# Products with the unit matrix in TensorE's waits, in a twelve-stage decoder

## The chip, the cores and the metric

The kernel runs on one core of a Trainium2 chip. The metric is device time in microseconds (us) of that core, the median of the runs; lower is better. TensorE (PE) multiplies matrices, VectorE (DVE), ScalarE (ACT) and GpSimd (POOL) compute elementwise and reduce, SyncE (SP) issues DMAs. Each engine works through its own list of instructions in order and waits on semaphores for the others.

## The reference

Four decoder layers over x, 64 sequences of 64 positions with 128 channels in float32, each of three parts with a residual. The parts differ from layer to layer:

```
x = x + _L0_attn_ref(_layernorm(x), ...)       # a0: differential attention
x = x + _L0_xattn_ref(ctx_1024, _layernorm(x)) # w0: dynamic time warping onto x
x = x + _L0_ffn_ref(_layernorm(x), ...)        # f0: three trees of experts, then attention
x = x + _L1_attn_ref(_layernorm(x), ...)       # a1: attention, 16 heads
x = x + _L1_xattn_ref(_layernorm(x), ctx_1024, ...)  # x1: attention with a gated memory
x = x + _L1_ffn_ref(_layernorm(x), ...)        # f1: mixture, top 2 of 8, and a shared expert
x = x + _L2_attn_ref(_layernorm(x), ...)       # a2: attention by pooled sums
x = x + _L2_xattn_ref(_layernorm(x), ctx_1024, ctx_1024, ...)  # x2: cross attention
x = x + _L2_ffn_ref(_layernorm(x), ...)        # f2: ternary weights
x = x + _L3_attn_ref(_layernorm(x), ...)       # a3: attention with relative bias
x = x + _L3_xattn_ref(_layernorm(x), ctx_1024, ctx_1024, ...)  # x3: restricted softmax
x = x + _L3_ffn_ref(_layernorm(x), ...)        # f3: routed experts, top 2 of 8
```

The middle of a1, as an example of an attention:

```
qkv = x @ Wqkv + bqkv
scores = jnp.einsum('bqhd,bkhd->bhqk', q, k) / jnp.sqrt(jnp.float32(HD))
attn = jax.nn.softmax(scores, axis=-1)
out = jnp.einsum('bhqk,bkhd->bqhd', attn, v).reshape(b, s, e)
return out @ Wout + bout
```

and of the mixture: `expert_values, expert_indices = jax.lax.top_k(router_probs, k=TOP_K)`, then each token's two experts and the shared one are added to x.

## The kernel before

x stays in SBUF as 32 tiles of 128 rows (NT = 32); four tiles make a group (GT = 4, NG = 8). The twelve stages run one after another, with a barrier of all engines between them, so a stage's time is that of its own longest chain. Within a stage each engine has one block of code, and the order of its work is the order in which the Python calls stand there. Nothing is scheduled at run time: what stands in front of an instruction on its engine delays it.

The five attentions are one function, `attention`. On PE it starts with turn_x(0) (L1081: four tiles of the normalised x against the unit matrix), make_q, make_k (L1087, L1091), with a bias two products more, turn_x(1), make_q(1), make_k(1), score(0) and make_v(0) (L1130, L1098). ACT copies each result from PSUM to SBUF before the next piece can use it. Then a loop over the 32 tiles i = 4 g + t: score(i + 1), early, turn(i) (L1141: eight tiles of softmax numerators into the banks TP), late, weigh(i) (L1154). DVE makes the maxima and differences (L843, L846) and the division (L824), ACT the exponentials and copies (L1016, L1021), which count pT_half up, twice in a tile. In a0 (`diff`) a per head norm is added: POOL's root (L699), then DVE's scaling with it (L797).

`memory_attention` (x1) goes through steps i of a group each: score, turn_weights, turn, weigh (L2498, L2499, into AV), project (L2456, L2461) and, in four steps, a part of the next stage's routing. `pooling` (a2) has in a step turn_q (L2751), total over C, logits (L2719, L2721), and total over B (L2759). `trees` (f0) turns x and scores the nodes of its trees batch by batch (L2015, L2023), places tokens with matrix products (L2041 to L2044), then runs the leaves and an attention over them. `ternary` (f2) starts with turn(0) and turn(1).

Both routings turn x, make logits (L3370 or L522), let DVE pick the best two, and call place (L3381 to L3384, L534 to L537), from whose sums DVE makes slots; POOL then scatters the rows to these slots in DRAM (L3119, L361), one indirect DMA for 128 rows. In f3 (`routed`) eight batches of four tiles are routed one behind another, then the groups of expert work follow. In f1 (`mixture`, class Router) there are four batches of eight tiles, the first two routed already in x1; the shared expert (do_shared L3779, yield_shared L3788, gelu on ACT L3737) runs on PE between them, and the expert groups follow.

## Time and profile before

| what | us |
|---|---|
| median of 3 runs (lowest, highest) | 2319.32 (2319.03, 2327.06) |
| span of the profiled execution | 2356.9 |
| PE busy (share of the span) | 1774.8 (75%) |
| DVE busy | 1337.8 (57%) |
| ACT busy | 1099.5 (47%) |
| POOL busy | 746.9 (32%) |

The stages end at these times of the profiled span, in us: a0 251.0, w0 395.3, f0 728.2, a1 907.7, x1 1045.2, f1 1316.1, a2 1453.5, x2 1618.2, f2 1696.7, a3 1896.3, x3 2060.6, f3 2356.9.

The profiled execution is 37.6 us longer than the median of the runs. Times of rows are from the start of its span. In a row of the timeline the second number is the duration, in brackets stands how long the engine had been idle before, and which work's end released it. A granted clock of 1.00 is 2.4 GHz on TensorE, 0.50 is 1.2 GHz.

### The profile page before, as it was taken

The numbers are of one execution on the slowest core, as the hardware profiler recorded it, in microseconds if no ns is written. First come the engines' busy times: TensorE is split into PE (matmuls) and PEld (weight loads), VectorE is DVE, ScalarE is ACT, GpSimd is POOL, SyncE is SP. The second block draws the span as 40 slices with busy tenths as digits, with TensorE's granted clock in tenths as the row PEclk, the third lists the DMA queues.
The fourth block names the chain that finished last, engine by engine and source line by source line (L and its number), as shares of the span: only waits on it lengthen the run. The fifth ranks groups of instructions, "written<-read, shape, count | busy, mean of one in ns | idle before, by whom it ended". The sixth has DMA issues, their size and how long they took to land. (4 is left out here: it accounts for less than half of the span.)

```text
span 2356.9 us, 39525 instructions
## 1 busy us (share of the span) xinstructions
PE 1774.8 (75%) x14484; PEld 1215.4 (52%) x14484; DVE 1337.8 (57%) x3646; ACT 1099.5 (47%) x2273; POOL 746.9 (32%) x718
## 2 busy tenths in 40 slices
PE   3887553999895996767999386887788868743994
PEld 1555432435543664644798253565555535542774
DVE  3897587502123774654343365885369969862223
ACT  4775531223243775733344243774357657610441
POOL 1223201360354331146255002330223232165453
PEclk9888885798896998877999697998979969955997
DMA  4111361125623301102376200000000010011224
GB/s 158 83 83 82 104 235 45 49 75 150 161 70 132 124 2 50 37 30 85 110 238 201 75 1 27 28 20 10 3 1 2 2 37 28 11 49 60 62 81 138
DMA packets 145170, 173.18 MB, mean 73 GB/s; under 512 B 21073, under 2 KB 120593, under 8 KB 144049
## 3 DMA queue, kind: packets, MB, share of 16 engines
q1 hardware_dynamic: 125252, 129.09, 17.7%
q0 software_dynamic: 13248, 28.21, 3.6%
q10 hardware_dynamic: 6480, 13.37, 1.5%
q8 instruction: 117, 1.92, 0.3%
q14 instruction: 73, 0.60, 0.1%
HBM read 126.84 MB, written 79.05 MB: 87 GB/s over the span
## 5 line engine op out<-in xcount | busy, mean ns | idle before, releaser
L1154 PE MATMUL a_AV<-a_vx,a_pT 128*64 128x18 f32 (+1 forms) x3072 | 115.1, 224 | 33.0 <-DVE a_two L824 15.3
L1154 PEld LDWEIGHTS a_AV<-a_vx,a_pT 128*64 128x64 f32 x3072 | 105.9, 146 | 62.2 <-issue 28.6
L1016 ACT ACTIVATE a_e<-a_e 128x512 f32<-128x512 f32 x192 | 110.2, 622 | 58.7 <-DVE a_e L846 58.5
L1141 PE MATMUL a_TP<-ident,a_e 128*128 128x128 f32 x768 | 108.0, 285 | 20.0 <-ACT a_e L1016 19.4
L1021 ACT COPY a_pT<-a_TP 128x512 f32<-128x512 f32 x192 | 103.4, 588 | 39.6 <-PE a_TP L1141 39.4
L846 DVE TENSOR_TENSOR a_e<-a_S,a_mx 128x1024 f32<-128x1024 f32 x96 | 117.3, 1222 | 2.9
L1141 PEld LDWEIGHTS a_TP<-ident,a_e 128*128 128x128 f32 x768 | 89.2, 146 | 57.6 <-ACT a_e L1016 48.3
L1130 PE MATMUL a_S<-a_kbd,a_qT 64*64 64x512 f32 x768 | 113.8, 668 | 0.9 <-issue 0.6
L3620 POOL DMA_INDIRECT f_back<-f_ys,f_row x78 | 74.7, 957 | 97.5 <-DVE f_ys L3709 85.6
L3126 POOL DMA_INDIRECT f_back<-f_ys,f_row x80 | 76.6, 957 | 87.1 <-DVE f_ys L3287 66.9
L3759 ACT ACTIVATE f_h<-f_H,f_wt 128x256 f32<-128x256 f32 x156 | 65.2, 473 | 83.5 <-PE f_H L3835 83.5
L843 DVE TENSOR_REDUCE a_mx<-a_S 128x16 f32<-128x1024 f32 x66 | 80.8, 1224 | 40.6 <-PE a_S L1130 39.4
L3352 ACT ACTIVATE f_h<-f_H,f_b 128x512 f32<-128x512 f32 (+1 forms) x96 | 56.5, 615 | 85.4 <-PE f_H L3445 78.6
L1948 ACT ACTIVATE f_h<-f_H,f_b 128x512 f32<-128x512 f32 x64 | 44.0, 687 | 103.1 <-PE f_H L2058 85.5
L1154 PE MATMUL x_AV<-x_vx,x_pT 128*64 128x18 f32 x2048 | 74.2, 215 | 23.7 <-ACT x_pT L1021 17.0
L843 DVE TENSOR_REDUCE x_mx<-x_S 128x16 f32<-128x1024 f32 x64 | 78.1, 1221 | 24.3 <-PE x_S L1130 24.0
L681 POOL TENSOR_TENSOR a_kbd<-a_kT,a_mask 128x512 f32<-128x512 f32 x64 | 64.5, 1039 | 81.1 <-ACT a_kT L991 81.1
L1154 PEld LDWEIGHTS x_AV<-x_vx,x_pT 128*64 128x64 f32 x2048 | 69.0, 142 | 37.2 <-issue 24.9
L1141 PEld LDWEIGHTS x_TP<-ident,x_e 128*128 128x128 f32 x512 | 58.4, 146 | 55.0 <-ACT x_e L1016 45.3
L1141 PE MATMUL x_TP<-ident,x_e 128*128 128x128 f32 x512 | 74.7, 290 | 15.5 <-ACT x_e L1016 15.4
L999 ACT ACTIVATE a_kbd<-a_kT,a_mask 128x512 f32<-128x512 f32 x128 | 85.6, 723 | 0.4
L671 POOL TENSOR_TENSOR a_rstd<-a_var,neghalf 128x4 f32<-128x4 f32 x24 | 24.3, 1014 | 187.7 <-DVE a_var L747 117.8
(544 smaller groups left out, 4731.4 us busy)
## 6 DMA issues: line engine op xcount, KB each, us to landing
f_wt<-in_f_ew SPq DMA_DIRECT2D x39, 584.0 KB
f_slots<-in_blank SPq DMA_DIRECT2D x1, 18576.0 KB
f_wt<-in_f_leaf SPq DMA_DIRECT2D x94, 98.0 KB, 2.0
f_xs<-f_slots SPq DMA_DIRECT2D x47, 144.0 KB
memory_x_k<-w_stage ACTq DMA_DIRECT2D x24, 256.0 KB, 3.2
f_slots<-in_blank SPq DMA_DIRECT2D x1, 5760.0 KB
f_xs<-leaf_slots SPq DMA_DIRECT2D x22, 256.0 KB
leaf_out<-f_ys SPq DMA_DIRECT2D x22, 256.0 KB
```

The source lines that it names most:

```text
L681: last = pool.tensor_tensor(kbd[:, n % 2, b:b + 2, 0:4, :], bc(kv[:, b:b + 2, :], 2, shape), mask8[:, 0:4].unsqueeze(1).unsqueeze(3).to_br ...
L843: return v.tensor_reduce(mx[:, i % 2, :], unit(i), AX.X, ALU.max)
L846: v.tensor_tensor(e[:, i % 2, :, :], unit(i), bc(mx[:, i % 2, :], 2, [P, NH, SL]), ALU.subtract).then_inc(shifted.sem, 1)
L999: last = act.activation(kbd[:, n % 2, :, h, :], keys(n).rearrange("p (b j) -> p b j", j=SL), ACT.Copy, scale=mask8[:, h:h + 1])
L1016: act.activation(eh, eh, ACT.Exp).then_inc(weights.sem, 1)
L1021: act.copy(pT[:, 4 * n:4 * n + 4, :], TP[:, n, :].rearrange("p (a b) -> p a b", a=4)).then_inc(pT_half.sem, 1)
L1130: last = pe.matmul(S[64 * c:64 * c + 64, i % 2, r, :], qT[rows, g % 2, SL * b:SL * b + SL], kbd[rows, g % 2, b, :, :], start=True, stop=True)
L1141: last = pe.transpose(TP[:, half, P * n:P * n + P], ev[:, 4 * half + n, :], k.ident[:, :])
L1154: last = pe.matmul(AV[64 * c:64 * c + 64, 2 * hp * W1:2 * (hp + 1) * W1], pT[:, hp, 64 * c:64 * c + 64], vx[:, g % 2, t, c, 2 * hp:2 * hp ...
L3126: pool.indirect_dma_start(out=back[:, :], out_offset=bass.IndirectOffsetOnAxis(ap=row[:, i % RR, t:t + 1], axis=0), in_=ys[:, i % RY, t, : ...
L3620: pool.indirect_dma_start(out=back[:, :], out_offset=bass.IndirectOffsetOnAxis(ap=row[:, i % RR, t:t + 1], axis=0), in_=ys[:, i % RY, t, : ...
L3759: act.activation(h[:, i % 2, c, 0:P * n], hid(i, c, n), ACT.Gelu_apprx_tanh, bias=weights(i)[2][:, c:c + 1])\
```

## The change

A helper, `keep_warm(pe, k, bank, n)`, multiplies the unit matrix by itself n times into the first 128 columns of a PSUM bank; nothing reads the result, and the next real product overwrites it. In float32 one such product is two PE instructions. It is called

- in the attentions: 17 products before turn_x(0) (not in a0), 2, 3, 3, 6, 2 and 3 between the first pieces (two of these calls only in the self attentions), 8 before turn(0); in a0 also 4 in each group at t == 1, behind a new wait for the first half of the step before's copies;
- in trees: 18 and 5 at the start, 5 and 5 in the first two batches, 5 in every late step of the attention over the leaves;
- in memory_attention: 24 at the start, 5 at the head of every weigh and 5 behind it;
- in pooling: 15 at the start, 3 in each step before the total over C; in ternary: 8 and 5;
- in routed, for f3: 10 before turn_x(0), 5 before the first logits, then 5 in front of turn_x, of place and of the next logits of each batch;
- in mixture, for f1: 14 before place(2), 30 before place(3).

Together these are 625 products, or 1250 instructions on PE.

```diff
--- before.py
+++ after.py
@@ -107,6 +107,12 @@
     if links:
         links.leave(n)
     body(NG - 1, (NG - 1) % 2, False, True)
+
+
+def keep_warm(pe, k, bank, n):
+
+    for _ in range(n):
+        pe.matmul(bank[:, 0:P], k.ident[:, :], k.ident[:, :], start=True, stop=True)
 
 
 def flat(ap):
@@ -1183,10 +1189,15 @@
                 if t == (2 if diff else 3) and not cross and g + 2 < NG:
                     make_k(g + 2)
 
+            if not diff:
+                keep_warm(pe, k, TP[:, 0, :], 17)
             turn_x(0, (xn_ready.sem, 1))
+            keep_warm(pe, k, TP[:, 0, :], 2)
             make_q(0, (xT_ready.sem, 1))
+            keep_warm(pe, k, TP[:, 0, :], 3)
             if not cross:
                 make_k(0)
+                keep_warm(pe, k, TP[:, 0, :], 3)
             if bias:
                 pe.wait_ge(setup_in.sem, n_setup)
                 for h in range(NH):
@@ -1200,8 +1211,12 @@
                 for n in range(2):
                     last = pe.matmul(S[:, 1, n, :], mt[:, 0:128], u[:, 8 * n:8 * n + 8, :], start=True, stop=True)
                 last.then_inc(bt_product.sem, 1)
+            if not cross:
+                keep_warm(pe, k, TP[:, 0, :], 6)
             turn_x(1, (q_ready.sem, 1) if cross else (v_ready.sem, 1))
+            keep_warm(pe, k, TP[:, 0, :], 2)
             make_q(1, (xT_ready.sem, 2))
+            keep_warm(pe, k, TP[:, 0, :], 3)
             if not cross:
                 make_k(1)
             if bias:
@@ -1212,6 +1227,11 @@
                 if i + 1 < NS:
                     score(i + 1)
                 early(g, t)
+                if i == 0:
+                    keep_warm(pe, k, TP[:, 0, :], 8)
+                if i and t == 1 and diff:
+                    pe.wait_ge(pT_half.sem, 2 * (i - 1) + 1)
+                    keep_warm(pe, k, TP[:, 0, :], 4)
                 turn(i)
                 late(g, t)
                 weigh(i)
@@ -2142,13 +2162,19 @@
 
             pe.wait_ge(setup_in.sem, 128)
             pe.wait_ge(k.f0_in, 32)
+            keep_warm(pe, k, HS, 18)
             turn_x(0)
             turn_x(1)
+            keep_warm(pe, k, HS, 5)
             for b in range(NBAT):
                 if b + 1 < NBAT:
                     turn_x(2 * b + 2)
                     turn_x(2 * b + 3)
+                if b < 2:
+                    keep_warm(pe, k, HS, 5)
                 score_nodes(b)
+                if b == 0:
+                    keep_warm(pe, k, HS, 5)
                 if b:
                     place(b - 1)
                 if b == 1:
@@ -2176,6 +2202,8 @@
                     score(scores_at[i])
                 if i in weights_at:
                     turn_weights(weights_at[i])
+                if m > NM:
+                    keep_warm(pe, k, H[:, 0, :], 5)
                 if i in values_at:
                     weigh(values_at[i])
     ph.close()
@@ -2489,6 +2517,7 @@
             def weigh(g):
                 if g:
                     pe.wait_ge(values_taken.sem, values_taken.after(g - 1))
+                keep_warm(pe, k, AV[:, 0, :], 5)
                 for t in range(GT):
                     if t == 0:
                         pe.wait_ge(ctx_in[g % 4].sem, ctx_in[g % 4].after(g // 4))
@@ -2499,6 +2528,7 @@
                     last = pe.matmul(out, eT[:, t, 1, :], cv[:, g % 4, t, :], start=False, stop=True)
                 last.then_inc(values.sem, 1)
 
+            keep_warm(pe, k, TP[:, 0, :], 24)
             pe.wait_ge(setup_in.sem, 16)
             for i in steps:
                 if within(i):
@@ -2513,6 +2543,8 @@
                     r.place(pe, batch[i - 4])
                 if within(i - 1):
                     weigh(i - 1)
+                if within(i - 1):
+                    keep_warm(pe, k, TP[:, 0, :], 5)
                 if within(i + 1):
                     project(i + 1)
                     make_gate(i + 1)
@@ -2758,6 +2790,7 @@
                         pe.wait_ge(*free)
                 pe.matmul(where[:, :], tri[:, :], w[:, n, :, :], start=True, stop=True).then_inc(sums[n].sem, 1)
 
+            keep_warm(pe, k, QKV[:, 0, :], 15)
             pe.wait_ge(setup_in.sem, 32)
             pe.wait_ge(bias_ready.sem, 2)
             for i in steps:
@@ -2775,6 +2808,7 @@
                     total(i, 0, B, (mT_ready.sem, mT_ready.after(i - 1)) if i else None)
                 if within(i + 1):
                     turn_q(i + 1)
+                    keep_warm(pe, k, QKV[:, 0, :], 3)
                 if within(i - 1):
                     total(i - 1, 1, C, (tail_ready.sem, tail_ready.after(i - 2)) if i >= 2 else None)
     ph.close()
@@ -2916,11 +2950,13 @@
                                          start=c == 0, stop=c == 3)
                 last.then_inc(product.sem, 1)
 
+            keep_warm(pe, k, H[:, 0, :], 8)
             turn(0)
             pe.wait_ge(ones_made.sem, 1)
             pe.wait_ge(abs_ready.sem, 1)
             pe.matmul(G[:, :], ones[:, :], ab[:, :], start=True, stop=True).then_inc(gamma_sum.sem, 1)
             turn(1)
+            keep_warm(pe, k, H[:, 0, :], 5)
             pe.wait_ge(ternary_ready.sem, 1)
             first_layer(0)
             for g in range(NG):
@@ -3403,14 +3439,20 @@
                 last.then_inc(sh_out.sem, 1)
 
             pe.wait_ge(setup_in.sem, n_early)
+            idle = 0 if shared else 5
+            keep_warm(pe, k, H[:, 0, :], 2 * idle)
             turn_x(0)
+            keep_warm(pe, k, H[:, 0, :], idle)
             make_logits(0)
             if shared:
                 pe.wait_ge(late_in.sem, n_late)
             for b in range(NBAT):
+                keep_warm(pe, k, H[:, 0, :], idle)
                 if b + 1 < NBAT:
                     turn_x(b + 1)
+                    keep_warm(pe, k, H[:, 0, :], idle)
                 place(b)
+                keep_warm(pe, k, H[:, 0, :], idle)
                 if b + 1 < NBAT:
                     make_logits(b + 1)
                 elif shared:
@@ -3796,11 +3838,13 @@
                 r.make_logits(pe, 2)
                 do_shared(1)
                 yield_shared(1)
+                keep_warm(pe, k, H[:, 2, :], 14)
                 r.place(pe, 2)
                 turn_batch(3)
                 r.make_logits(pe, 3)
                 do_shared(2)
                 yield_shared(2)
+                keep_warm(pe, k, H[:, 2, :], 30)
                 r.place(pe, 3)
                 count_all()
                 for n in range(3, NSH):
```

## Rows read from the trace of the kernel before

**Rows 1.** Cores: the span and the mean granted TensorE clock.

```profile
core 0: 2356.9 us, clock 0.857
```

**Rows 2.** Windows: length, busy us (instructions) of PE, PEld, DVE, ACT, POOL; clock, DMA.

```profile
736.90:755.20 18.30, 12.47 (x28) 5.24 (x28) 3.34 (x15) 7.33 (x13) 5.86 (x6) 0.50 0.50 216
1462.40:1473.40 11.00, 8.60 (x24) 3.24 (x28) 7.62 (x16) 5.67 (x11) 8.69 (x10) 0.51 0.14 48
1705.00:1729.10 24.10, 20.61 (x68) 10.18 (x72) 4.73 (x17) 9.61 (x16) 6.01 (x7) 0.50 0.00 1
1905.50:1914.00 8.50, 6.13 (x12) 2.43 (x12) 6.96 (x15) 3.40 (x7) 6.19 (x7) 0.50 0.19 62
```

**Rows 3.** Timeline, PE, second attention: start, us, work [idle before <-releaser].

```profile
736.93 1.09 PE L1081 MATMUL a_PJ<-ident,a_xn 128*128 128x128 f32 x4 [12.57 <-ACT a_xn L962]
...
744.46 2.08 PE L1098 MATMUL a_PJ<-mats,a_xT 128*128 128x128 f32 x8 [0.78 <-ACT a_kT L991]
...
757.61 1.16 PE L1098 MATMUL a_PJ<-mats,a_xT 128*128 128x128 f32 x8
```

**Rows 4.** Windows of PE alone, trees and pooling's start: length, busy us, clock.

```profile
418.30:421.80 3.50, 3.50 (x22) 0.50 0.00 0
421.80:425.20 3.40, 3.30 (x34) 0.99 0.00 0
1323.80:1330.70 6.90, 5.93 (x28) 0.57 0.00 0
```

**Rows 5.** Timeline, PE, mixture: the shared expert.

```profile
1102.00 3.78 PE L3779 MATMUL f_H<-f0w 128*128 128x512 f32 x4 [9.34 <-ACT f_h L3737]
...
1106.56 6.10 PE L3788 MATMUL f_Y<-f0w,f_h 128*128 128x128 f32 x32 [0.78 <-ACT f_h L3737]
...
1117.26 3.84 PE L3788 MATMUL f_Y<-f0w,f_h 128*128 128x128 f32 x32 [0.78 <-ACT f_h L3737]
```

**Rows 6.** Timeline, PE, POOL and DVE, first attention.

```profile
33.08 2.08 PE L1098 MATMUL a_PJ<-mats,a_xT 128*128 128x128 f32 x8 [0.68 <-ACT a_kT L989]
...
99.01 1.18 PE L1141 MATMUL a_TP<-ident,a_e 128*128 128x128 f32 x8 [1.38 <-ACT a_e L1016]
...
105.72 5.43 POOL L699 TENSOR_TENSOR a_hs<-a_hs,neghalf 128x32 f32<-128x32 f32 x1 [4.79 <-DVE a_hs L793]
...
106.93 1.22 DVE L843 TENSOR_REDUCE a_mx<-a_S 128x16 f32<-128x1024 f32 x1 [1.12 <-PE a_S L1130]
...
111.25 0.69 DVE L797 TENSOR_TENSOR a_att<-a_raw,a_hs 128x512 f32<-128x512 f32 x1 [0.26 <-POOL a_hs L699]
```

**Rows 7.** Timeline, PE and ACT, memory attention.

```profile
942.58 0.46 PE L2498 MATMUL x_AV<-x_nv,x_eT 128*128 128x129 f32 x2 [1.32 <-ACT x_eT L2418]
...
944.44 1.88 PE L2456 MATMUL x_PJ<-x_nT,mats 128*128 128x512 f32 x4
...
947.70 0.49 ACT L2364 ACTIVATE x_raw<-x,x_nmr,x_root 128x128 f32<-128x128 f32 x1 [0.74 <-DVE x_up L2279]
...
953.70 0.46 PE L2498 MATMUL x_AV<-x_nv,x_eT 128*128 128x129 f32 x2 [2.10 <-ACT x_eT L2418]
...
956.70 1.54 PE L2456 MATMUL x_PJ<-x_nT,mats 128*128 128x512 f32 x2
```

**Rows 8.** Timeline, PE, pooling: the same piece in four steps.

```profile
1332.48 0.66 PE L2751 MATMUL a_A<-ident,a_qkv 128*128 128x128 f32 x4 [1.85 <-DVE a_qkv L2600]
...
1373.43 0.66 PE L2751 MATMUL a_A<-ident,a_qkv 128*128 128x128 f32 x4 [0.99 <-DVE a_qkv L2600]
...
1385.90 0.66 PE L2751 MATMUL a_A<-ident,a_qkv 128*128 128x128 f32 x4 [0.99 <-DVE a_qkv L2600]
...
1428.79 0.66 PE L2751 MATMUL a_A<-ident,a_qkv 128*128 128x128 f32 x4 [0.99 <-DVE a_qkv L2600]
```

**Rows 9.** Timeline, PEld and POOL, routed stage.

```profile
2065.19 0.72 PEld L3362 LDWEIGHTS f_PJ<-ident,f_pay 128*128 128x128 f32 x4 [6.60 <-DMA f_tri<-in_tri_all]
...
2076.64 1.06 POOL L3119 DMA_INDIRECT f_slots<-f_pay,f_slot  x1 [9.08 <-DVE f_slot L3220]
```

## The prediction

> **What bounds the kernel now.** I read three views, in this order. First the core's own line: a span of 2356.9 us with TensorE at a mean granted clock of 0.857 [rows 1]. The record knows two levels, 2.4 GHz (1.00) and 1.2 GHz (0.50), so a mean of 0.857 means that about 0.143 x 2 x 2356.9 = 674 us of the span ran at the lower one. Second the windows at the starts of stages: there the clock is 0.50 to 0.57 while PE is busy for much of the stretch, 12.47 of 18.3 us in the second attention, 20.61 of 24.1 us in the one with a bias [rows 2, 4]. Third the timeline of such a start: PE had waited 12.57 us for the normalised x, then the first transposes run slowly, and the same eight instructions of the v projection take 2.08 us at the lower level and 1.16 us at the upper one 13 us later [rows 3]. So no single engine bounds the kernel: each stage begins with a serial chain (normalise, turn, project, copy, score, softmax) in which PE's pieces alternate with short copies, and those pieces are on the path at half the clock. After it DVE, ACT or PE bounds the loop.
>
> What raises the clock: in the tree stage PE is busy without a gap at 0.50 in 418.3 to 421.8 us, with 22 instructions, 14 of which multiply by the unit matrix, and in the next stretch the clock is 0.99 [rows 4]. Short pieces with the unit matrix therefore do seem to count. By the Trainium skill's page "TensorE: Matmul & The Clock Gate", Part 4, the full clock doesn't engage for transposes; the trace shows the clock rising behind a stretch made mostly of them, and what the change adds are plain products anyway. If I followed that page for them, they would be pure cost (that outcome is the first rival).
>
> **The price of one product.** Two PE instructions of 128 columns each. Warm: 32 such instructions take 3.84 us [rows 5], 16 products, so 0.24 us each. Cold: 0.24 x 2.08 / 1.16 = 0.43 us [rows 3, 5]. The change issues 625 products: 59 + 44 + 44 in the three self attentions, 35 + 35 in the two cross ones, 78 in the trees, 104 in the memory attention, 44 in the mixture, 39 in the pooling, 13 in the ternary stage, 130 in the routed one. All at the upper level they are 150 us of PE's time, at the lower 269 us; what matters is which of them stand in front of work.
>
> **The starts of the attentions.** Second attention: 17 products are issued before turn_x(0), which is 7.3 us if all are cold, inside 12.57 us in which PE waits [rows 3]. They cost nothing, and by then the clock should be up. The work behind then runs at the upper level: 12.47 us of PE at 0.50 [rows 2], times 1 - 1.16/2.08 = 0.44, and nearly half for longer pieces, saves 5.5 to 6.1 us. The further products (2, 3, 3, 6, 2, 3, 8) stand in waits of 0.7 to 2 us for ACT's and DVE's copies; warm they are 0.5 to 1.9 us each, and the longest pokes out by a few tenths. Net +5.5. With the bias: 20.61 us busy at 0.50 [rows 2] give 9 to 10; the 6 products before turn_x(1) stand where PE hardly waits (about 1.4 us). Net +8.5. First attention, which has no 17: the same pieces at the lower level (2.08 us for the v projection [rows 6]; the record has no clock event that early), a longer wait before; +3.5, since its pieces alternate with a mask product and a copy that don't change. Cross attentions: 8.60 and 6.13 us busy at 0.50 [rows 2], so 3 to 4 us each, plus about 1 of the first steps of their loops, less 0.5 for products that poke out: +4 each. Lower bound for all these: nothing, if the clock falls back in what is left of the wait (after the 17 products 2 to 5 us of it remain). Upper bound: everything on the path, 44 to 50% of the rows.
>
> **The loop of the first attention.** In seven of its eight groups PE works for some 7 us at the lower level behind a wait. The 4 products at t == 1 stand in the 1.38 us wait for the softmax before the transposes [rows 6], so at 0.96 us they are hidden. The new wait on pT_half guards the bank that they write and counts the step before, so it has long been met; queued behind it are turn(i) and weigh(i), for which DVE and ACT wait. What is gained is small: DVE waited 1.12 us for slow scores, but POOL's root that runs beside it takes 5.43 us, and DVE's head scale then waits 0.26 us for it [rows 6]. If the scores come 1.1 us earlier, that wait grows to nearly 1.4. I keep 0.35 us per group: +2 to +2.5 for seven. Bounds: 0 and 7 x 1.5 = 10. With the start +5.5.
>
> **The memory attention.** Every weigh now has 5 products in front (1.2 us warm), in a wait of 2.10 us for ACT's copy: hidden. weigh takes 1.86 us warm (942.58 to 944.44) and 3.00 us cold (953.70 to 956.70) [rows 7], so a cold step gives 1.1 us back, and in the rest of the step as much again at most; some five steps are cold. The second 5 stand directly before project(i+1) with no wait: 1.2 us later, of which ACT has 0.74 us to spare [rows 7], so about 0.45 us lost in each of seven. The last weigh comes after a long wait and pays its 5 cold, 2.1 us. Gain 5 x 1.6 = 8, cost 3.2 + 2.1, start +1: +4 (bounds -6 and +9).
>
> **Trees, pooling, ternary.** Trees: the 18 products lie in a wait of over 10 us but end about 2 us after x could be turned; ACT's normalisation runs on until then. Everything to 421.8 ran at 0.50 [rows 4], yet DVE's decisions bound part of it; +3 (bounds -4 and +7). Pooling: the start has 5.93 us at a clock of 0.57 [rows 4], +2.4. The steady step is 12.47 us (1373.43 to 1385.90), but the seven steps from 1332.48 to 1428.79 take 96.31, 9.0 us over 7 x 12.47 [rows 8]; in the slow ones the clock had fallen. The 3 products (0.72 us) fill the wait of about 0.7 us before the second total and should keep it up; I take 3.6 of the 9: +6 (bounds 0 and 11). Ternary: +1.5 (bounds -2 and +3), the same reasoning at a sixth of the size.
>
> **The mixture.** 14 and 30 products stand before place(2) and place(3), where PE works through the shared expert; 44 x 0.24 = 10.6 us in front of work that bounds the stage. Against them: PE idles 9.34 us at 1102.00 before the next piece, and the second product behind it takes 6.10 us instead of 3.84 [rows 5]. Part of the 30 may fall into that idle time, if what ends it isn't itself behind place(3). But ACT and DVE both seem to wait for PE there, place(3)'s slots among it, so I count it as mostly lost: -6.5 (bounds -12 and +5).
>
> **The routed stage.** 10 products before turn_x(0), whose weight load waited for the landing of a setup load until 2065.19 us [rows 9]: 3.5 to 4.3 us late, with 5 more in front of the logits and of place(0); the pieces between are warm then and give 2 us back. POOL's first scatter is at 2076.64 [rows 9], and POOL bounds the next 90 us with eight batches of scatters, so this delay of its start stays to the end, while the products of the later batches (about 115) lie in PE's waits. -2 (bounds -5 and +1).
>
> **The sum.** 5.5 + 5.5 + 8.5 + 4 + 4 + 4 + 3 + 6 + 1.5 - 6.5 - 2 = 33.5 us. It is made against the profiled 2356.9 us; the median of the runs, 2319.3 us, is 37.6 us less because they carry no profile, and I take the saving over as it is: 2319.3 - 33.5 = 2285.8, so 2286 us. The terms' errors together are some 18 us either way: 2268 to 2304.
>
> **The rivals.**
> (1) Slower: products with the unit matrix don't lift the clock. For: no stretch of this trace consists of such products alone. Against: [rows 4]. The starts would then keep their clock, and each product that stands in front costs 0.43 us less its wait: three self attentions 27 products each, 11.6 less about 7 us of waits, 14 us together; cross 6; memory attention 13; trees 8; pooling 6; mixture 11; routed 5: about 63 us, 2380 us. Between its -63 and the forecast's +33.5 the point from which it decides is a third of the stretches: it is even where the clock is lifted in only two of three. Chance 0.10.
> (2) The starts bring half: the clock falls again between the products' end and x's arrival, or DVE and ACT bound the start once PE is quicker. Then the gross gains, 47 us with the memory attention's 9 before its costs, become 23.5, and the costs of memory attention, mixture and routed stage, 13.8, stay: 2319.3 - 9.7 = 2309.6, between 2304 and 2322. For: of the 12.57 us of wait [rows 3] some 5 are left behind the 17 products. The Trainium skill's page "TensorE: Matmul & The Clock Gate", Part 1, says that for modelling the ramp is under 1% of a typical kernel's span; that would be under 24 us here and about 2305 us with the mixture's cost. The trace has 674 us at the lower level, so I don't follow it. Chance 0.16.
> (3) The mixture's 30 products fall into PE's idle 9.34 us and save the slow piece behind it [rows 5]: 2286 - 10 = 2276, between 2262 and 2280. Chance 0.14.
> (4) The forecast: 0.60.
>
> **How the numbers follow.** Range: 2264 to 2316 leaves out (1), the far part of (2) and a little of (3), under 2 in 10. What a measurement of this kernel can tell from no change is about 0.5%, 11.6 us: faster is below 2307.7, slower above 2330.9. Faster: 0.60 + 0.14 and the better part of (2), 0.03, less 0.01: 0.76. Slower: 0.10 and a little for unseen delays, 0.11. Same: 0.13.
>
> **What would show it right or wrong.** In the profile after: the starts of the attentions at a clock of 1.00, with the v projection at 1.16 us; the mean granted clock up from 0.857 to above 0.9; memory attention's and pooling's steps even; DVE's head scale waiting over 1 us for POOL; the mixture's next piece behind place(3) later than 1102 us relative to the stage's start, and its shared expert's end some 7 us late; POOL's first scatter of the routed stage about 2 us later from the stage's start. The forecast is wrong if a start still shows 0.50 behind its products (then rival 1 or 2), or if a stage without a cold stretch grows by more than its products in front.

## The result, and the profile after

The changed kernel takes 2307.8 us (median of five runs, 2305.3 to 2309.9) against 2319.3 us; the ratio of the runs is 0.9943, with a 95% interval of 0.9924 to 0.9962. Timed again beside two other kernels it stood at 0.9912 (0.9887 to 0.9937), so the gain is between 9 and 26 us, most likely 12 to 20. The prediction was 2286 us, a gain of 33.5 us: the direction is right, the size is about two to three times too large.

The core's line, which answers [rows 1], of the changed kernel:

```profile
core 0: 2303.5 us, clock 0.909
```

The same line of the kernel before, profiled a second time:

```profile
core 0: 2324.1 us, clock 0.864
```

The span of either is about 2 us below the time of its own run (2305.3 and 2326.1 us). The 2356.9 us of [rows 1] were therefore not the usual time with a cost of profiling on top, as the prediction took them; that one execution was longer than the repeated one, by 22 us in the tree stage, 10 us in the mixture and 7 us in the memory attention. No run tells why. All comparisons of stages below use the repeated profile and those of the variants. A stage's length is here the time from VectorE's first instruction in it to its first in the next:

```
us                   a0     w0     f0     a1     x1     f1     a2     x2    f2     a3     x3     f3
before, repeated   230.7  145.6  311.4  186.1  125.4  262.2  139.2  164.5  78.5  200.0  165.2  295.1
after              229.0  145.3  306.0  180.7  123.5  268.5  130.2  161.1  79.1  196.3  164.5  298.9
after, repeated    228.0  146.2  306.2  177.8  125.1  271.5  131.0  160.9  79.1  196.3  163.0  296.6
starts only        229.8  145.9  310.2  177.8  127.2  260.0  137.1  164.0  77.7  195.2  164.3  295.4
```

The same code mostly differs by 1 to 4 us from one profile to the next (pooling by up to 6, and the trees without any products by more: 306.5, 311.4 and once 333.1 us), so a single difference of 2 us says little; a1 and x1 are best read together, since DVE's first instruction of x1 waits for a load.

Three readings of the changed kernel. First, the windows over the four starts of [rows 2] (length, busy PE, PEld, DVE, ACT, POOL, clock, DMA):

```profile
708.50:726.00 17.50, 15.71 (x102) 11.10 (x103) 6.73 (x18) 11.38 (x20) 9.70 (x10) 1.00 0.52 222
1412.70:1423.00 10.30, 9.85 (x56) 6.59 (x57) 8.41 (x17) 6.53 (x12) 7.98 (x9) 0.84 0.17 51
1651.60:1675.00 23.40, 21.85 (x117) 14.29 (x118) 5.78 (x18) 10.75 (x18) 7.28 (x8) 0.78 0.00 1
1848.40:1858.00 9.60, 8.46 (x56) 5.52 (x57) 7.91 (x16) 6.52 (x12) 7.29 (x8) 1.00 0.18 56
```

The clock was 0.50 in all four. It is now 1.00 in the second attention and in x3, but 0.84 and 0.78 in the other two: there it fell again. Second, the timeline of the second attention's start, which answers [rows 3]:

```profile
700.64 6.56 PE L115 MATMUL a_TP<-ident 128*128 128x128 f32 x34 [5.00 <-PEq L158]
708.58 0.63 PE L1087 MATMUL a_PJ<-ident,a_xn 128*128 128x128 f32 x4 [1.38 <-ACT a_xn L968]
...
713.91 1.16 PE L1104 MATMUL a_PJ<-mats,a_xT 128*128 128x128 f32 x8
```

Products with the unit matrix do raise the clock: after 5.00 us without work PE runs 34 instructions and nothing else for 6.56 us, the clock goes from 0.50 to 1.00 while they run, and the four real ones 1.38 us later take 0.63 us where they had taken 1.09; the v projection takes 1.16 us at once. These are plain products; whether transposes alone would do the same was not tried. Third, the mixture, which answers [rows 5]:

```profile
1051.67 6.86 PE L115 MATMUL f_H<-ident 128*128 128x128 f32 x60
1058.37 0.19 PE L540 MATMUL f_H<-f1r_sel,f1r_tri 128*128 128x64 bf16 x1
...
1058.63 3.87 PE L3821 MATMUL f_H<-f0w 128*128 128x512 f32 x8
```

PE goes from the products to place(3) and on to the shared expert without a gap; they stand fully in front of it.

### The profile page after: what moved, and what is told of

Its sections match the earlier page's. It is cut to its first block and busy times, and to the rows that moved or that the text cites. A ratio compares the mean times of both kernels' runs of the same rounds, so it can differ in the third digit from the quotient of the medians.

```text
span 2303.5 us, 42024 instructions
## 1 busy us (share of the span) xinstructions
PE 1857.6 (81%) x15734; PEld 1339.0 (58%) x15734; DVE 1337.9 (58%) x3646; ACT 1102.6 (48%) x2273; POOL 748.4 (32%) x718
## 5 line engine op out<-in xcount | busy, mean ns | idle before, releaser
L1136 PE MATMUL a_S<-a_kbd,a_qT 64*64 64x512 f32 x768 | 108.3, 638 | 0.3
L115 PE MATMUL f_H<-ident 128*128 128x128 f32 x454 | 77.7, 338 | 7.4 <-DMA f_tri<-in_tri_all 5.6
```

What stands on the lines that cost most here:

```text
L115: pe.matmul(bank[:, 0:P], k.ident[:, :], k.ident[:, :], start=True, stop=True)
L1136: last = pe.matmul(S[64 * c:64 * c + 64, i % 2, r, :], qT[rows, g % 2, SL * b:SL * b + SL], kbd[rows, g % 2, b, :, :], start=True, stop=True)
```

## The experiments

**The kernel before, unchanged, profiled again.**

> The unchanged kernel before, to see what of its first profiled execution is its own. Theory A (the prediction's): the profile itself adds the 37.6 us, so this profiled span is again near 2357 us and its tree stage again near 333 us. Theory B: the first profiled execution was an unusual one; this span is 1 to 3 us below the time of its run (2313 to 2325 us), the tree stage is 22 to 30 us shorter than 333 us, and the clock is still near 0.86. Only against this profile can the terms be read stage by stage. Timed against itself its ratio should hold 1.000.

Measured: ratio 0.9998 (0.9982 to 1.0014); span 2324.1 us, tree stage 311.4 us, clock 0.864. Theory B. A difference of 0.2% can be told from none in this comparison. And in the mixture the idle 9.34 us of [rows 5] is gone:

```profile
1062.38 3.84 PE L3788 MATMUL f_Y<-f0w,f_h 128*128 128x128 f32 x32 [0.78 <-ACT f_h L3737]
1066.05 0.19 PE L534 MATMUL f_H<-f1r_sel,f1r_tri 128*128 128x64 bf16 x1
...
1066.31 3.87 PE L3779 MATMUL f_H<-f0w 128*128 128x512 f32 x8
```

Here place(3) (1066.05) is followed by eight products of the shared expert in one piece; there is nothing in which 30 products could hide.

**Only the starts.** All calls at the starts of the attentions (17, 2, 3, 3, 6, 2, 3, 8), trees (18, 5, 5, 5), memory attention (24), pooling (15) and ternary (8, 5); the others are taken out:

```diff
@@ weigh, memory_attention
-                keep_warm(pe, k, AV[:, 0, :], 5)
...
@@ mixture
-                keep_warm(pe, k, H[:, 2, :], 14)
...
-                keep_warm(pe, k, H[:, 2, :], 30)
```

> Only the products at the starts of stages (first pieces of the attentions, trees, memory attention, pooling, ternary); none in loops, in either routing or in the mixture, and without the new wait. Theory A: the starts bring nearly all the gain and what stands in the routings and loops costs (the prediction had -8.5 for mixture and routed stage, about -3 in the memory attention): 10 to 18 us below the changed kernel's time less pooling's loop (3 to 6 us), so about 2298 us. Theory B: the starts' warm pieces are paid back by a later fall of the clock, and half or more of the measured 11.5 us came from the loops of memory attention and pooling: about 2314 us.

Measured: 0.9903 (0.9880 to 0.9926), 2300.8 us. That is nearer to theory A (2298 us) than to B (2314 us), and the starts bring all the gain that can be seen: against the 0.9943 of the first timing they do better alone, against the 0.9912 of the second the two are the same. By stages, the mixture falls back to 260.0 us and the routed stage to 295.4, while pooling loses most of its gain (137.1).

**Only the rest**, the complement with a0's wait.

> The complement: only the products in loops (first attention at t == 1 with its wait, trees' late steps, memory attention's weigh and behind it, pooling's step), in the routed stage's routing and in the mixture. Theory A: a loss of 0 to 5 us against before, about 2321 us. Theory B: a gain of 5 to 8 us, about 2313 us. If parts of different stages only add, its change and that of the starts alone sum to -11.5 us within 4 us.

Measured: 1.0022 (1.0005 to 1.0039), 2326.3 us: about 5 us slower than before. The two ratios' changes add to -0.75%, -17 us, inside what the two timings of the changed kernel span. The products outside the starts were, by themselves, a loss. The stages of this profile show one place that the whole hides: the first attention, which here has its loop's products and the new wait but not the start's, took 233.5 us, against 230.4 to 231.4 in three profiles without any.

**Only those ahead of the first turn.**

> Only the products ahead of the first turn of a stage (17 in four attentions, 18 in trees, 24 in memory attention, 15 in pooling, 8 in ternary), none between the pieces. Theory A: they raise the clock and the pieces keep it up alone (in the kernel before PE is busy 12.47 of 18.3 us there): 80% of what the starts give. Theory B: at full speed the pieces fill too little of the time, the clock falls again within the start, and less than half of it is left; the second attention's start then shows 0.50 in its second half.

Measured: 0.9980 (0.9963 to 0.9997), 2318.7 us, a fifth of what the starts give: theory B. The timeline of the second attention's start shows it:

```profile
716.11 1.16 PE L1104 MATMUL a_PJ<-mats,a_xT 128*128 128x128 f32 x8 [0.78 <-ACT a_kT L997]
719.20 1.12 PE L1087 MATMUL a_PJ<-ident,a_xn 128*128 128x128 f32 x4 [1.93 <-DVE a_vx L783]
721.08 2.05 PE L1093 MATMUL a_PJ<-a_xT,mats 128*128 128x512 f32 x2 [0.77 <-ACT a_xT L978]
```

The v projection is still fast; after the next wait of 1.93 us the four transposes take 1.12 us, and what follows runs at the lower level for 10.2 us. With the few products in the short waits the same start stayed at 1.00 (the window of the changed kernel above), so they are what held the clock. That it falls without them because the real pieces are only half as long at the upper level, and the same waits weigh more, is my reading; no run varied it.

**The starts and pooling's loop** (`keep_warm(pe, k, QKV[:, 0, :], 3)` back in).

> The starts and pooling's three products in each step: what a stage by stage reading of the profiles so far leaves as worth having. Theory A (stages only add; in the changed kernel's profile pooling is 9.0 us shorter than in the repeated profile of before, with the starts alone 2.1 us): 5 to 7 us below the starts alone, ratio to before 0.987 to 0.989, about 2293 us. Theory B (the clock falls elsewhere instead, so that a loop's products give nothing that lasts): the same as the starts alone, ratio 0.990.

Measured: 0.9913 (0.9895 to 0.9931), 2297.7 us. By ratio the same as the starts alone, so theory B for the whole, though the two were timed in different comparisons and 7 us, 0.3%, would fit into their intervals. By the stage it is theory A: pooling is again 130.2 us instead of 137.1, as in four other profiles with its start's and its loop's products (130.2 to 131.0; a fifth has 133.1). The two pay only together: with the start's alone pooling takes 137.1 us, with the loop's alone 136.6, with neither 139.2 and 137.2.

**Only the mixture's 44.**

> Only the mixture's 14 and 30 products. Theory A (the prediction's term, which took PE's idle 9.34 us before L3779 for real): 6.5 us slower than before, ratio 1.003, with part of the 30 inside PE's idle time. Theory B (the repeated profile shows no such idle time, place(3) is followed at once): each product costs its full 0.22 us, less what the shared expert's slow pieces get back: 6 to 9 us slower, ratio 1.003 to 1.004, and the stage 268 to 270 us against 262.2 in the repeated profile. Theory C (the time hides behind the scatters of POOL): no change, 1.000.

Measured: 1.0063 (1.0042 to 1.0084), 15 us slower; the stage took 273.2 us, 11 more than in the repeated profile of before. Theory B in kind, though above its size of 6 to 9 us: nothing is hidden, and nothing comes back. What made the whole 4 us worse than the stage stays open.

**A longer start for the attention with a bias.** What had gone wrong there is to be seen in the changed kernel's timeline:

```profile
1645.82 1.95 PE L115 MATMUL a_TP<-ident 128*128 128x128 f32 x16
1651.63 1.09 PE L1087 MATMUL a_PJ<-ident,a_xn 128*128 128x128 f32 x4 [3.86 <-ACT a_xn L968]
...
1657.85 1.97 PE L1204 MATMUL a_S<-a_mt,a_relT 32*32 32x64 f32 x32
1659.75 1.16 PE L1104 MATMUL a_PJ<-mats,a_xT 128*128 128x128 f32 x8
1661.58 3.72 PE L1212 MATMUL a_S<-a_u,a_mt 32*128 32x512 f32 x4 [0.67 <-ACT a_u L1064]
1665.23 2.93 PE L115 MATMUL a_TP<-ident 128*128 128x128 f32 x12
```

The 17 products end 3.86 us too early and the first transposes are slow again (1.09 us). Later the clock falls a second time (at 1661.67 us), although PE has waited only 0.67 us: before it stand L1204's 32 small products, 32 rows by 32 columns of the array, then the v projection on the whole array (L1104, still fast) and that wait. L1212 then takes 3.72 us, and the 6 products behind it, meant to help, take 2.93 us instead of 1.5 on the path. The edit:

```diff
-                keep_warm(pe, k, TP[:, 0, :], 17)
+                keep_warm(pe, k, TP[:, 0, :], 26 if bias else 17)
@@ behind the products of L1204
                 last.then_inc(u_product.sem, 1)
+                keep_warm(pe, k, TP[:, 0, :], 6)
@@ before turn_x(1)
-                keep_warm(pe, k, TP[:, 0, :], 6)
+                keep_warm(pe, k, TP[:, 0, :], 0 if bias else 6)
@@ in the loop
+                if cross and i in (1, 2):
+                    pe.wait_ge(pT_half.sem, 2 * (i - 1) + 1)
+                    keep_warm(pe, k, TP[:, 0, :], 5)
```

> As the starts with pooling, but in the attention with a bias 26 products in place of 17 before turn_x(0), and the 6 before turn_x(1) moved to behind the bias's first, 32-row products (L1204); in the cross attentions also 5 products before turn(i) in tiles 1 and 2. Theory A (the bias attention got 3.7 of the 8.5 us because the clock fell twice in its start, once in the 3.86 us left behind the 17 products and once in the stretch of 32-row products): the start now stays at 1.00, L1212's products take 1.9 instead of 3.7 us, and the stage is 3 to 4 us shorter than with the starts alone (195.2 us), 191 to 192 us. Theory B (its start is bound by DVE and ACT): 194 to 196 us. In the cross attentions the clock stays up behind the start: 1.5 us less in each by A; nothing by B, since DVE bounds the loop.

Measured: the stage with a bias took 191.4 us (195.2 to 196.3 in six profiles without the edit; the two runs further on that keep it have 192.2 and 190.7), theory A; the whole 0.9885 (0.9868 to 0.9902), 2293.0 us, 4.6 us below the starts with pooling in the same comparison. Its timeline:

```profile
1648.94 0.63 PE L1087 MATMUL a_PJ<-ident,a_xn 128*128 128x128 f32 x4 [1.84 <-ACT a_xn L968]
...
1650.53 2.04 PE L1093 MATMUL a_PJ<-a_xT,mats 128*128 128x512 f32 x2 [0.51 <-ACT a_xT L976]
...
1655.27 1.97 PE L1204 MATMUL a_S<-a_mt,a_relT 32*32 32x64 f32 x32
1657.17 1.60 PE L115 MATMUL a_TP<-ident 128*128 128x128 f32 x12
1658.62 1.06 PE L1104 MATMUL a_PJ<-mats,a_xT 128*128 128x128 f32 x8
1659.60 1.98 PE L1213 MATMUL a_S<-a_u,a_mt 32*128 32x512 f32 x4
```

The same six products, two pieces earlier, take 1.60 us, and the product that took 3.72 us takes 1.98. The second fall is absent in all three profiles with the edit and present in all six with the starts but without it. The start did not stay at 1.00 throughout, as theory A had it: the first transposes are fast (0.63 us), but then the clock is at 0.50 for 3.4 us, and the first q projection takes 2.04 us. The 26 products and the moved six were not tried apart. In the cross attentions the extra products brought nothing (165.2 and 164.4 us, not less than the 160.9 to 164.5 and 160.1 to 164.5 us without them), theory B.

**The memory attention's products at the head of weigh** (on top of the starts and pooling).

> As the starts with pooling, and the memory attention's 5 products at the head of every weigh, without the 5 behind it. Theory A (the prediction: those at the head are hidden in the wait for ACT's copy and give 1.6 us in each of five cold steps): the stage 4 to 7 us shorter than with the starts alone (127.2 us). Theory B (in the changed kernel the stage's cold time fell from 40 to 14 us and its length by only 2.0 us, so its steps are bound by ACT, DVE and POOL): 125 to 127 us.

Measured: 0.9892 (0.9874 to 0.9910), 2292.7 us; the stage 125.9 us against 126.5 to 127.2 in four profiles without them. Theory B: one microsecond, not 1.6 in each of five steps.

**Pooling's tail.**

```diff
@@ pooling, in the loop over steps
+                if i == NG - 1:
+                    keep_warm(pe, k, QKV[:, 0, :], 8)
                 if within(i):
                     total(i, 0, B, ...)
...
+                if i == NG:
+                    keep_warm(pe, k, QKV[:, 0, :], 16)
                 if within(i - 1):
                     total(i - 1, 1, C, ...)
```

> The starts and pooling's products, the longer start of the attention with a bias from the run before, without the cross attentions' extra ones, and new in pooling: 8 products before the second last step's total over B and 16 before the last total over C, since the last 18 us of that stage ran at 0.50 in each profile. Theory A (the tail's pieces are on the path): pooling 2 to 4 us below 130.3 us. Theory B (at the tail DVE's chain bounds, and PE's wait is too long to be bridged): 130 us or up to 2 us more. The whole in either case 2289 to 2294 us, ratio 0.986 to 0.989.

Measured: 0.9837 (0.9812 to 0.9862), 2284.6 us, the best version of all and below the 2289 to 2294 us of both theories; pooling 126.4 us, theory A. Two lines of the changed kernel's tail, then the same pieces here:

```profile
1389.49 1.06 PE L2759 MATMUL a_B<-ident,a_mixed 128*128 128x128 f32 x4
1391.24 2.07 PE L2751 MATMUL a_L<-a_lb,a_ones 1*128 1x512 f32 x2 [0.69 <-ACT a_mT L2720]
```

```profile
1379.03 1.95 PE L115 MATMUL a_QKV<-ident 128*128 128x128 f32 x16
...
1383.86 0.60 PE L2760 MATMUL a_B<-ident,a_mixed 128*128 128x128 f32 x4
1385.15 1.12 PE L2752 MATMUL a_L<-a_lb,a_ones 1*128 1x512 f32 x2 [0.69 <-ACT a_mT L2721]
```

The wait for ACT is the same 0.69 us in both; the pieces around it take half the time.

**Without the routings.** The changed kernel without the mixture's 44 and the routed stage's 130.

> The changed kernel without its products in the mixture (44) and in the routed stage (130). Theory A (they cost 8 to 9 and 3 us and give nothing back): mixture 260 to 262 us, routed stage 295 to 296 us, the whole 10 to 12 us below the changed kernel's, 2296 us, ratio 0.989 to 0.990. Theory B (their cost is hidden, and the difference between stages is chance from one execution to the next): within 4 us of the changed kernel, ratio 0.993 to 0.995.

Measured: 0.9876 (0.9851 to 0.9902), 2293.6 us, 9.4 us less than the changed kernel timed beside it. Theory A: mixture 258.1, routed stage 296.3 us.

**The changed kernel again.**

> The changed kernel unchanged, beside the two others, for its ratio and a second profile. Theory A: ratio 0.994 as first measured, mixture 267 to 270 us and routed stage 298 to 299 us again; pooling 130 us. Theory B (the single profiles of stages are chance): mixture or routed stage within 1.5 us of the kernels without their products (262 and 295.5 us).

Measured: 0.9912, 2303.0 us; mixture 271.5, pooling 131.0, routed stage 296.6 us. The ratio is nearer to 0.991 than to the 0.994 expected. Theory A for the mixture and pooling. For the routed stage it is between the two: 298.9 once, 296.6 now, 298.5 in the run of only the rest, 295.1 to 296.3 in ten profiles without its products.

**The memory attention with a start long enough.** The changed kernel's start there:

```profile
876.61 7.22 PE L115 MATMUL x_TP<-ident 128*128 128x128 f32 x48 [1.74 <-PEq L158]
888.09 1.09 PE L2474 MATMUL x_PJ<-ident,x_nv 128*128 128x128 f32 x4 [4.26 <-DVE x_nv L2313]
```

The 24 products are followed by 4.26 us of nothing, and the first turn is slow.

> The best version so far (starts, pooling with its tail, longer start of the attention with a bias) with the memory attention's products: 5 at the head of every weigh and 5 behind it as in the changed kernel, but 40 in place of 24 at its start. In the changed kernel's profile the 24 end 4.26 us before the first turn, which then runs at 1.09 us, the slow time. Theory A (the start gave nothing because the clock had fallen again): the first turn now takes 0.66 us, L2484's first four products about 2.0 instead of 3.8 us, and the stage is 2.5 to 4 us shorter than in the two profiles of the changed kernel (124.3 us), 120 to 122 us; the whole 3 to 6 us below the version without, ratio 0.981 to 0.983. Theory B (DVE, ACT and POOL bound this stage from its first piece on): 124 to 126 us and a ratio of 0.984.

Measured:

```profile
878.53 11.93 PE L115 MATMUL x_TP<-ident 128*128 128x128 f32 x80 [1.73 <-PEq L158]
890.29 0.60 PE L2475 MATMUL x_PJ<-ident,x_nv 128*128 128x128 f32 x4
...
893.21 2.49 PE L2485 MATMUL x_PJ<-x_nT,mats 128*128 128x512 f32 x4 [1.88 <-ACT x_xT L2417]
```

The first turn takes 0.60 us, L2485 2.49 us; the stage 122.3 us, 2.0 us below the mean of the changed kernel's two profiles (1.2 us if a1 and x1 are read together): between the theories. The whole did not follow: 0.9861 (0.9844 to 0.9879), 2288.1 us, no better than without; pooling, whose code is the same, took 132.1 us in this profile instead of 126.4, its clock at 0.50 for 23.5 us instead of 13.8. It seems that what is saved in one stage shifts where the clock falls in the next ones; with one profile of each this is not shown.

## Why the prediction was wrong

The mechanism was right: the clock is up (0.857 and 0.864 before, 0.909 after), unit products raise it, and rival 1 is refuted by the timeline of the second attention. [rows 4] alone had not shown it: right before that stretch, without a gap, stand L2023's 16 products on other data (414.45 to 417.7 us). The sum was wrong. What the stages gain before the costs of mixture and routed stage is about 28 us, where the prediction had 42; the step that failed is that PE's busy time at 0.50, times 0.44 to 0.5, was counted in full as time of the stage. The measured 2307.8 us lie in the range of rival 2 (2304 to 2322), which had a chance of 0.16, and both of its causes occurred. Its terms against the means over the profiles with and without a stage's products (in us, gain positive; each measured one is uncertain by 1 to 2):

```
                              predicted   measured
first attention                   5.5        2.0
trees                             3          3 (304.7 to 311.4 without some of them: uncertain)
second and memory attention       5.5 + 4    5.4 together
mixture                          -6.5      -10
pooling                           6          7.4
cross attentions x2, x3           4 + 4      3.4 + 2.5
ternary                           1.5        0.5
attention with a bias             8.5        3.7
routed stage                     -2         -2.4
sum                              33.5       15.5
```

**The attention with a bias (8.5, measured 3.7)** is the largest miss. The step that failed is "20.61 us busy at 0.50 give 9 to 10": it took every busy microsecond of [rows 2] to be one that would run at the upper level. Two things broke it. The lower bound the prediction named itself, a clock that falls in what is left of the wait, happened (3.86 us left). And busy was taken to be enough: behind L1204's small products, the v projection and a wait of 0.67 us the clock fell with PE at work. The run with 26 products and the six moved brought back 4 us of the 4.8 missed, so these two together account for it.

**The mixture (-6.5, measured -10)** failed at "part of the 30 may fall into that idle time". The idle 9.34 us were in one execution only. The price itself (0.24 us a product, 10.6 us) was right (the 30 took 6.86 us, 0.23 each) and should have stood undiminished. The runs with the 44 alone (+11 us in the stage) and without them (258.1 us) show it from both sides; rival 3 is refuted.

**The first attention (5.5, measured 2.0).** The start did as predicted: the first turn in the loop, released by ACT's exponentials, came 3.75 us earlier in the span than in the first profile of before (47.31 for 51.06 us) and 4.0 us earlier than in the repeated one. But little of the loop's +2 to +2.5 came. The rows for the loop, DVE's piece L792 a group later each time, with DVE's head scale in the second group and the windows of the two groups:

```profile
94.88 0.68 DVE L792 TENSOR_REDUCE a_hs<-a_raw 128x32 f32<-128x512 f32 x1
...
119.17 0.67 DVE L792 TENSOR_REDUCE a_hs<-a_raw 128x32 f32<-128x512 f32 x1
...
132.22 0.69 DVE L803 TENSOR_TENSOR a_att<-a_raw,a_hs 128x512 f32<-128x512 f32 x1 [1.36 <-POOL a_hs L705]
...
142.84 0.67 DVE L792 TENSOR_REDUCE a_hs<-a_raw 128x32 f32<-128x512 f32 x1
```

```profile
90.00:114.00 24.00, 21.59 (x228) 14.02 (x227) 21.20 (x45) 16.95 (x33) 7.18 (x4) 0.86 0.19 82
114.00:138.00 24.00, 19.27 (x234) 13.04 (x231) 21.59 (x47) 17.73 (x33) 7.91 (x4) 1.00 0.19 81
```

In the first group the four products did not hold the clock (0.86, as before) and the group took 24.29 us; in the second they did (1.00) and it took 23.67, against 23.9 in the steady groups of the kernel before. So even a group wholly at the upper level gains only about 0.25 us of the 0.35 predicted; the 24.29 us are within what groups without products take (up to 24.5). The limit is the one that the prediction took from [rows 6]: DVE's wait for POOL's root, 0.26 us before, is 1.36 us in the fast group, as it had said (nearly 1.4). What it had not foreseen is the end of the loop. From one piece L792 to the next, the sixth interval takes 23.3 to 23.5 us in the four profiles with the loop's products and 22.1 us in all ten without them, so 1.3 us are lost there; the seventh takes 19.6 us with them and 18.4 or 20.0 without. Which part of it is the products and which the new wait was not tried apart.

**The memory attention (4, measured nearly 0).** "Start +1" failed because the 24 products ended too early; 40 in their place brought 2.0 us. 1.6 us in each of five cold steps was too much: the stage's time at 0.50 fell from 39 us to 14 and 17 us in the changed kernel's two profiles, yet its length by 1 us. Which engine then holds the steps was not tried alone.

**The cross attentions (8, measured 5.9)**: x3's start kept the clock at 1.00, but behind the 8 products at i == 0 came a wait of 2.43 us, and 1.5 us after its end the clock fell for 10 us, where before it had fallen for 7:

```profile
1857.06 2.05 PE L115 MATMUL x_TP<-ident 128*128 128x128 f32 x16
1861.54 1.18 PE L1147 MATMUL x_TP<-ident,x_e 128*128 128x128 f32 x8 [2.43 <-ACT x_e L1022]
1862.96 1.85 PE L1160 MATMUL x_AV<-x_vx,x_pT 128*64 128x18 f32 x32 [0.25 <-ACT x_pT L1027]
```

DVE's first maximum came 1.7 us earlier in the stage and no longer waited for PE: DVE's own work, here the next group's normalisation (L757), now stands in front. The first row is the changed kernel's, the second the repeated profile's of before:

```profile
1857.48 1.22 DVE L849 TENSOR_REDUCE x_mx<-x_S 128x16 f32<-128x1024 f32 x1
```

```profile
1882.94 1.23 DVE L843 TENSOR_REDUCE x_mx<-x_S 128x16 f32<-128x1024 f32 x1 [1.75 <-PE x_S L1130]
```

This is rival 2, in part. Its first cause, a clock that falls before x arrives, occurred in three starts: the attention with a bias, the memory attention and x2 (2.53 us left, first transposes 1.09 us); its second, that another engine is next, in x3.

**Pooling and the routed stage** came out as reckoned. In the routed stage PE began its ten products only when the setup load had landed, 4.6 us at the lower level, and POOL's first scatter came 17.4 us after its first instruction of the stage instead of 15.5. The first two rows are the changed kernel's, the others the repeated profile's of before:

```profile
2004.51 0.21 POOL L3134 MEMSET f_ones<- 128x128 f32 x1 [38.46 <-POOLq L158]
...
2021.92 1.06 POOL L3155 DMA_INDIRECT f_slots<-f_pay,f_slot  x1 [10.99 <-DVE f_slot L3256]
```

```profile
2028.95 0.21 POOL L3098 MEMSET f_ones<- 128x128 f32 x1 [37.47 <-POOLq L152]
...
2044.45 1.06 POOL L3119 DMA_INDIRECT f_slots<-f_pay,f_slot  x1 [9.09 <-DVE f_slot L3220]
```

**The sentence on profiling (37.6 us)** was wrong, as told above. It did little to the sum, since the terms were read locally, but two of the rows it rested on, the mixture's idle time and its slow piece, belonged to that execution.

**The rule of the page "TensorE: Matmul & The Clock Gate"** of the Trainium skill that I set aside, that the ramp is worth under 1% of a typical span (Part 1), came nearer to the changed kernel than my sum did: 0.6 to 0.9% here. The best version stands at 1.6% all the same, so it is no bound for this kernel.

## What to carry to other kernels

Filler work on an engine pays only where the engine provably waits for another one, in every execution: look for the wait in two profiles, and make the filler last until the real work arrives, since 2.3 to 4.3 us left over undid it in 15 of 25 starts here, and short waits between pieces need their few products too. Before counting a slow stretch as gain, ask of each piece in it whether its speed moves the engine that holds the stage; in a loop where VectorE waited for GpSimd, a clock of 1.00 instead of 0.86 was worth 1%. Wherever filler stands in front of a busy engine (the mixture), its full price is paid, and it took back 10 of the 28 us that the other stages had gained.

## What the runs showed of the hardware

- 34 instructions that multiply the unit matrix by itself, and nothing else, took the clock from 0.50 to 1.00.
- Fast pieces and short waits can lose the clock again: in the attention with a bias, behind 32 products on a 32 by 32 part of the array (1.97 us), eight on the whole array (1.16 us) and a wait of 0.67 us, the next product ran at the lower level (3.72 us). With six full products behind the 32, and a longer start, it did not (1.98 us). Whether the small part of the array or the wait counted more was not told apart.
- Between the unit products' end and a stage's first transposes, over the six kinds of start that had 15 products or more and all profiles with them: with up to 2.23 us without work the clock was still at 1.00 in all 30 cases, with 2.31 to 4.27 us in 10 of 25, with 5.6 us and more in none of 5. The same code lands on either side: x2 was at 0.50 after 2.31 us in one profile of the changed kernel's start, at 1.00 after 4.27 us in another with the same products. A clock still up at the first transposes can fall within the start: 1.3 us after their start in the attention with a bias with 26 products.
- The same code gave a stage of 126.4 and 132.1 us (pooling with its tail) and of 160.9 and 164.5 us (x2), with the clock at 0.50 at different places and for different lengths. That this is the whole cause was not shown. A difference of 2 us in one stage of one profile is within it.
